# Where a softmax is divided: on TensorE and VectorE after the weighing, or on GpSimd before the transposes

## The reference

```
x  = x + attention(layernorm(x) -> q, k, v; mask 1) @ w_ao + b_ao
x  = x + attention(layernorm(x) -> q; context -> k, v; mask 2) @ w_co + b_co
x  = x + gelu(layernorm(x) @ w1 + b1) @ w2 + b2
attention: scores = q k^T / sqrt(32);  scores = scores * mask - 10000 * (1 - mask)
           probs = softmax(scores);  out = probs @ v        (16 heads of 32 channels)
```

## Time and profile before

| | us |
|---|---|
| median of three runs | 1862.97 |
| span of the profiled execution | 1856.0 |
| PE busy (share of the span) | 1736.2 (94%) |
| DVE busy | 1216.0 (66%) |
| ACT busy | 1071.9 (58%) |
| POOL busy | 99.5 (5%) |

### The profile page before, as it was taken

The page is one execution under the profiler, slowest core; times in us unless marked ns, Lnnn a source line. Parts: engine busy times, 40 slices in busy tenths (PEclk is TensorE's granted clock), DMA queues, the critical chain, the costliest instruction groups (busy, mean ns, idle before and its releaser), DMA issues.

```text
span 1856.0 us, 34276 instructions
## 1 busy us (share of the span) xinstructions
PE 1736.2 (94%) x12832; PEld 1244.6 (67%) x12832; DVE 1216.0 (66%) x2792; ACT 1071.9 (58%) x2333; POOL 99.5 (5%) x79
## 2 busy tenths in 40 slices
PE   4879999999999988999999989999999889999999
PEld 2324343444434333788888878888888779999998
DVE  5666776767776552488887887888887753333332
ACT  2346666756666574587778777777777731111111
POOL 1110101101000000000000000000000000000000
PEclk7779999999999898999999999999999999999999
DMA  6322223222222222566656766666665340000000
GB/s 160 120 82 61 91 85 97 69 92 89 81 70 66 80 61 85 140 160 167 173 149 177 196 170 189 175 174 174 172 166 154 114 144 23 23 24 23 26 28 16
DMA packets 168334, 201.73 MB, mean 109 GB/s; under 512 B 25573, under 2 KB 115813, under 8 KB 168169
## 3 DMA queue, kind: packets, MB, share of 16 engines
q1 hardware_dynamic: 167880, 199.14, 38.2%
q10 hardware_dynamic: 288, 0.39, 0.1%
HBM read 131.84 MB, written 67.63 MB: 107 GB/s over the span
## 4 chain that ended last, share of the span: by engine, by line
PE 81%; DVE 9%; ACT 5%; issue 2%; DMA 1%; DVEq 1%; ACTq 0%; SPq 0%; POOL 0%
PE c_d L2099 10%; PE c_sums L2114 9%; PE b_d L1361 9%; PE b_d L1373 9%; PE a_d L501 6%; PE b_d L1440 5%; PE a_escore L472 5%; PE a_d L579 3%; PE a_d L571 3%; PE a_mscore L484 3%; PE b_score L1428 3%; PE a_d L555 3%; PE b_d L1457 3%; DVE a_mx L804 2%; PE a_d L563 2%
## 5 line engine op out<-in xcount | busy, mean ns | idle before, releaser
L804 DVE TENSOR_REDUCE a_mx<-a_mscore 128x2 f32<-128x1024 f32 x247 | 301.9, 1222 | 170.6 <-PE a_mscore L484 169.2
L641 ACT ACTIVATE a_pt<-a_escore 128x1024 f32<-128x1024 f32 x256 | 262.5, 1025 | 164.2 <-PE a_escore L472 163.7
L1590 ACT ACTIVATE b_pr<-b_t,b_nmax 128x256 f32<-128x256 f32 x512 | 254.4, 501 | 124.7 <-DVE b_nmax L1766 124.7
L1762 DVE TENSOR_TENSOR b_t<-b_score,b_mask 128x1024 f32<-128x1024 f32 x128 | 155.1, 1212 | 85.6 <-PE b_score L1428 85.2
L2198 ACT ACTIVATE c_gT<-c_d,c_b 128x256 f32<-128x256 f32 x128 | 53.7, 472 | 267.4 <-PE c_d L2099 267.4
L1766 DVE CUSTOM_DVE_ANT_0 b_t<-b_t,b_minus 128x256 f32<-128x256 f32 x512 | 187.5, 422 | 16.8
L472 PEld LDWEIGHTS a_escore<-a_qst,a_kst 50*128 50x128 f32 x512 | 49.9, 191 | 180.7 <-ACT a_pt L641 106.1
L472 PE MATMUL a_escore<-a_qst,a_kst 50*128 50x512 f32 x512 | 133.2, 516 | 24.9 <-ACT a_pt L641 23.9
L2243 DVE CAST c_g_high<-c_gT 128x512 fp32r<-128x512 f32 x64 | 40.2, 629 | 172.0 <-ACT c_gT L2198 172.0
L2099 PE MATMUL c_d<-c_ln_high,c_w_high 128*128 128x256 f32 x512 | 144.7, 283 | 2.3 <-DVE c_ln_low L2245 2.3
L2099 PE MATMUL c_d<-c_ln_high,c_w_low 128*128 128x256 f32 x512 | 144.9, 283 | 0.0
(11 more groups left out here) (165 smaller groups left out, 3271.3 us busy)
## 6 DMA issues: line engine op xcount, KB each, us to landing
b_qst<-b_q SPq DMA_DIRECT2D x96, 256.0 KB, 4.8
b_kst<-b_k SPq DMA_DIRECT2D x96, 256.0 KB, 6.4
b_q<-b_qparts SPq DMA_DIRECT2D x64, 256.0 KB, 4.5
b_k<-b_kparts SPq DMA_DIRECT2D x64, 256.0 KB, 3.4
a_qst<-a_q_parts SPq DMA_DIRECT2D x192, 64.0 KB, 2.2
a_kst<-a_k_parts SPq DMA_DIRECT2D x186, 64.0 KB, 2.2
a_k_parts<-a_kparts SPq DMA_DIRECT2D x32, 256.0 KB, 2.3
a_q_parts<-a_qparts SPq DMA_DIRECT2D x32, 256.0 KB, 2.3
```

Of the source, the lines that this page charges most:

```text
L641: nc.scalar.activation(pt[:, at % RING, :, :], escore[:], ACT.Exp, scale=SCALE).then_inc(exp_done.sem, 1)
L804: nc.vector.tensor_reduce(mx[:, q, 2 * pair:2 * pair + 2], maxima_bank(b, n)[:], AX_X, ALU.max).then_inc(max_done.sem, 1)
L1590: last = nc.scalar.activation(pr[:, u % 2, j, :], t[:, u % 2, j, :], ACT.Exp, scale=-1.0, bias=nmax[:, u, j:j + 1], accum_out=esum[:, u, j ...
```

## The change

`divide` no longer divides, and `weigh` no longer spreads the reciprocals. Instead POOL multiplies the exponentials of each unit by the reciprocal of their row's sum, in place in `pr`, before PE transposes them. PE's transposes now wait for this (`weights_done`) and not for the exponentials. `invert` moves from the end of a DVE position to its start: invert(p+1) now stands ahead of soften(p+2). A placeholder keeps the SBUF layout as it was.

```diff
@@ gpsimd
-            for v in range(LAST + 1):
-                rsqrt(v + 2)
+            def weights(v, u):
+                if not there(v):
+                    return
+                pool.wait_ge(inverse_done.sem, inverse_done.at(v, u + 1))
+                nc.gpsimd.tensor_tensor(pr[:, u % 2], pr[:, u % 2], inverse[:, u, :].unsqueeze(2).broadcast_to([P, G, S]),
+                                        ALU.mult).then_inc(weights_done.sem, 1)
+
+            def position(v, p):
+                if p == 1:
+                    rsqrt(v + 2)
+                weights(*unit_at(v, p + 1))
...
@@ tensor, turn_probs
-                pe.wait_ge(exp_done.sem, exp_done.at(v, u + 1))
+                pe.wait_ge(weights_done.sem, weights_done.at(v, u + 1))
@@ tensor, weigh
-                for x in range(2):
-                    u = 2 * pair + x
-                    pe.wait_ge(inverse_done.sem, inverse_done.at(v, u + 1))
-                    for j in range(G):
-                        mm = nc.tensor.matmul(at[j * DH:(j + 1) * DH, (2 + x) * P:(3 + x) * P],
-                                              inverse[:, u, j:j + 1].broadcast_to([P, DH]), ident[:],
-                                              start=True, stop=True, tile_position=(0, j * DH))
@@ vector, divide
-                nc.vector.tensor_copy(spread[:], at[:, 2:4, :])
-                nc.vector.drain()
-                nc.vector.tensor_tensor(cx[:, 2 * h:2 * h + 2, q * P:(q + 1) * P], at[:, 0:2, :], spread[:],
-                                        ALU.mult).then_inc(cx_done.sem, 1)
+                nc.vector.tensor_copy(cx[:, 2 * h:2 * h + 2, q * P:(q + 1) * P], at[:, 0:2, :]).then_inc(cx_done.sem, 1)
@@ vector, position
             def position(v, p):
+                invert(*unit_at(v, p + 1))
                 soften(*unit_at(v, p + 2))
...
-                invert(*unit_at(v, p + 1))
```

More of the change, by code:

```diff
@@ L1004, in attention_layer @@
         cxp = sb("cxp", [P, 2, KT, S], F32R)
-        spread = sb("spread", [P, 2, P])
+        sb("over_ident", [P, 2 * P])
         masks_ = [[sb(n + "1", [P, TT, S])] for n in ("mask", "minus")]
@@ L1076, in attention_layer @@
         inverse_done = sig("inverse_done", NU)
+        weights_done = sig("weights_done", NU)
         cx_done = sig("cx_done", NU // 2)
@@ L1339, in _ @@
             nc.gpsimd.memset(ones[:].bitcast(F32), 1.0).then_inc(bias_set.sem, 1)
-            for v in range(LAST + 1):
-                rsqrt(v + 2)
+            def weights(v, u):
[8 more added lines that the diff above has]
+                weights(*unit_at(v, p + 1))
+            weights(0, 0)
+            for v in range(END):
+                for p in range(NU):
+                    position(v, p)
+            second["gpsimd"] = position
         @block.tensor
@@ L1456, in weigh @@
                             head = (h * HH + four * G + j) * DH
-                            nc.tensor.matmul(at[j * DH:(j + 1) * DH, x * P:(x + 1) * P], val[v % 2][:, k, head:head + DH],
-                                             pt[:, slot(v, u), k, j * P:(j + 1) * P],
-                                             start=(k == 0), stop=(k == TT - 1), tile_position=(0, j * DH))
-                for x in range(2):
-                    u = 2 * pair + x
-                    pe.wait_ge(inverse_done.sem, inverse_done.at(v, u + 1))
-                    for j in range(G):
-                        mm = nc.tensor.matmul(at[j * DH:(j + 1) * DH, (2 + x) * P:(3 + x) * P],
-                                              inverse[:, u, j:j + 1].broadcast_to([P, DH]), ident[:],
-                                              start=True, stop=True, tile_position=(0, j * DH))
+                            mm = nc.tensor.matmul(at[j * DH:(j + 1) * DH, x * P:(x + 1) * P], val[v % 2][:, k, head:head + DH],
+                                                  pt[:, slot(v, u), k, j * P:(j + 1) * P],
+                                                  start=(k == 0), stop=(k == TT - 1), tile_position=(0, j * DH))
                 mm.then_inc(pv_done.sem, 1)
@@ L2056, in _ @@
         def _(pool):
+            ahead = second["gpsimd"]
+            for p in range(4):
+                ahead(END, p)
             pool.wait_ge(consts_in.sem, 16 * 5)
@@ L2059, in _ @@
             nc.gpsimd.drain()
+            ahead(END, 4)
             def steps(b, first=False):
@@ L2064, in steps @@
                 nc.gpsimd.tensor_tensor(rstd[:], vare[:], half[:].broadcast_to([P, TT]), ALU.pow).then_inc(rstd_done.sem, 1)
+                if first:
+                    for p in range(5, POSITIONS):
+                        ahead(END, p)
                 pool.wait_ge(xn_done.sem, xn_done.at(b, 1))
```

## The result

The changed kernel takes **1985.62 us** (median of 4 runs, 1984.55 to 1986.25) against 1863.7 for the kernel before on the same chip (4 runs, 1859.38 to 1864.87): a ratio of 1.0661, 95% interval 1.0644 to 1.0677, so 122 us slower. 2013 was forecast, range 1955 to 2075.

A forecast was written before the change was run, and what follows sets the result against it. PE bounds the kernel before; afterwards a DVE-ACT loop does: 127 x 6.14 = 780, plus 35 and 19, makes 834 against 683.6, +150. Span 1856.0 becomes 2006, plus 7 gives 2013 us, range 1955 to 2075.

The forecast's parts named there:

- The loop: Part b: early reciprocal makes DVE's masking and reductions and ACT's exponentials work in turn, 5.04 us a unit without contention.
- The block: DVE's reductions, reading two SBUF inputs, are held until POOL's multiplication ends; the loop becomes 6.14 us a unit.
- E + 2.70: End of POOL's multiplication, counted from E, the end of a unit's exponentials: 0.30 us to its start plus 2.40.
- 6.14: Microseconds a unit takes in the DVE-ACT loop with reductions held by POOL; counted 127 times, 780 us.
- worse: takes longer: Rival, chance 0.15: POOL's in-place multiplication takes longer than 2.40 us; at 3.40, 2140 us in total.
- not near 2.4 us: Sign of being wrong: POOL's multiplication, priced at 2.40 us, has another duration.
- Late unit 2: POOL multiplies unit 2 only after `rsqrt`, which waits for DVE's variance: 2.5 us a round, 14 rounds, 35 us.
- the contested place: DVE's reductions for unit 4 meet POOL's ready product of unit 3; POOL going first costs 2.5 us a round, otherwise 0.9.
- PE's clock and late scores: After idling for unit 2, PE runs at its lower clock and scores come late: 0 to 1.8 us a round, taken as 0.
- Rounds of the same length: Sign in the profile after: self and cross rounds both about 51 us, since PE no longer sets their length.
- Weight splits: In five places `invert` stands behind the splitting, which joins the loop: 3.8 us each, 19 us.
- The spreading matmuls' 28 us: PE drops 64 pairs x 0.44 = 28 us of spreading matmuls, worth nothing because PE then waits.

The follow-up runs named there:

- x_loop: Kernel before, with only `invert` moved from the end of a DVE position to its start, no product on POOL: 1880.68 us, ratio 1.0096.
- x_half: Changed kernel, with POOL multiplying only 2 of the 4 heads of a unit, the others left undivided: 1943.8 us, ratio 1.0434.
- x_three: Changed kernel, with POOL multiplying 3 of the 4 heads of a unit, one left undivided: 1956.3 us, ratio 1.0500.
- x_rsqrt: Changed kernel, with POOL at position 1 multiplying unit 2 ahead of `rsqrt` and not behind it: 1947.77 us, ratio 1.0458.
- x_last: Changed kernel, with `invert` back at the end of the DVE position, POOL still dividing: 2035.53 us, ratio 1.0924.
- x_last_look: x_last run once more with nothing changed, for a trace at PE's usual clock: 2036.08 us.

## Why the prediction was right, and where its terms were off

- **The loop** (5.04 us unblocked): right. x_loop's steps are 5.03 to 5.07 where nothing else is in the way, and in the changed kernel, where the scores and so the masking come late and POOL is through before the reductions, the next step is 5.07 in most rounds.
- **The block**: right in kind, shown by x_half and x_three. **Its size was off**: I took 2.40 us from an addition whose two inputs both advance along the row and read it as good "also with a broadcast input"; but there a row of 512 values is used twice, while here one value stands for 256, and the product takes 1.90. That makes E + 2.20 in place of E + 2.70, and the step came out at 5.62 in place of 6.14, and 127 x 0.52 = 66 us less than forecast. No rival had a price below 2.40 ("worse: takes longer"), and the 0.3 us of error that I allowed for the 6.14 is less than these 0.52. An operation "not near 2.4 us" was one of my signs of being wrong, and it came.
- **Late unit 2**: the order at the contested place is right (POOL first). I forecast 2.5 us a round over regular steps, but self rounds are 48.4 to 49.8 against 8 x 5.62 = 45.0, so 3.4 to 4.8 us. The missing part is **PE's clock and late scores**, which I named, priced at 0 to 1.8 us and then set to 0. Of the 2.96 us that the masking at 1056.33 waits, the slower matmuls make 2.7, and 1.5 us in the round with the step of 9.06. x_rsqrt takes the whole place away and gains 38 us.
- **Rounds of the same length**: wrong. The five cross rounds from the second on take 265.7 us, so 53.1 each, 8.2 over regular steps. PE still sets their first step, by its wait for `b_encp` ahead of the q projection (2.87 us at 1288.88) and by what the projection then takes. That step was 7.80 us before, longer than 6.14 even then, which the average of 5.4 us a position hid; the lower clock and the held reduction bring it to 9.83.
- **Weight splits**, 3.8 us each: too high. The steps with a split are 11.11, 10.12, 8.84, 8.29 and 8.81 us. Two of them are 3.2 and 2.7 over a regular one, the first and the last lie in steps that are long without a split, and 10.12 is 4.0 over the 6.15 of that place, but the late unit 2 of the same round then costs next to nothing (5.95 in place of 9 to 10.5). In this one, at 1095.58, the splitting itself (two SBUF inputs) meets unit 2's product and takes 4.05 us in place of 2.36. It holds POOL up too, which takes 2.75:

```profile
1095.58 4.05 DVE L1695 TENSOR_TENSOR b_wq<-b_stage,b_wq 128x1024 fp32r<-128x1024 f32 x2
```

- **Sum.** 127 x 5.62 = 713.7, so what is not a regular step is 809.5 - 713.7 = 95.8 us, where 35 + 19 = 54 were forecast. So -66 and +42 make -24 of the 27 us between 2013 and 1985.6. The other 3 are what is left of two things: the span outside of the maskings grew by 2.5 us, and the median lies 1.2 us over the profiled span, not the 7 that I added. Two errors of opposite sign made the total look better than its terms; that much of it was luck.
- **The spreading matmuls' 28 us are worth nothing once PE waits**: borne out, though no run changes them alone. x_loop, which keeps them, and x_half, which has them not, make the same regular step (5.05 and 5.05 to 5.09). PE's busy time went up by 25 us in the changed kernel (1736.2 to 1761.7), though it has fewer matmuls to do; the rows at the lower level above are the only longer ones I found.

What stays open: that x_loop's 16 us and the rest add up is not shown: the terms share the same waits, and x_last shows that taking one away can cost more than it gives.

## What to carry to other kernels

Moving work to an idle engine cost latency twice here, in its own chain and in what it blocks. What I would try, from this one case: before doing it, add up the chain from one issue of the bounding engine to the next through the new engine (here scores to product, 4.94 us), and compare it with the *shortest* position that engine now makes (3.48), not with the mean (5.2). An engine that is busy all the time can still lose 7% by the order of its list, since others live on what it gives early. When an engine will have to stand still once a round, count what it then does at the lower clock.

## What the runs showed of the hardware that was not expected

- GpSimd's in-place multiplication with one input broadcast along the row (stride 0) takes 1.90 us for 128x1024 fp32, 1.47 for 128x768 and 1.04 for 128x512. That is about 0.18 us + 1.68 ns per value of a row, an estimate from the first and last that gives 1.47 for the second. The addition of 128x1024 with both inputs advancing along the row took 2.40; no run changes the stride alone, so that the stride makes the difference is not shown.
- Two GpSimd operations that are both ready let VectorE make one short instruction in between (3.92 us for the two, the next reduction 2.10 us in place of 0.42). Held the other way, behind a VectorE instruction with two SBUF inputs, the same product takes 2.75 to 2.92 us. The Trainium skill has this exclusion ("SBUF — State Buffer", "Who interferes with whom"); the trace agrees also for VectorE's custom reduction, 0.99 us against 0.42.
- The transposes that follow 5.61 us of idle TensorE take 1.97 us, and those after 4.08 us in x_last_look too, against 1.04: the lower level and the upper. Behind shorter idle stretches both occur. In x_rsqrt the q projection follows 3.01 us of idle time in rounds 8 to 14, and takes 3.11 us at a granted clock of 1.00 in one of them, 4.27 to 5.46 at 0.67 to 0.50 in the others; in x_loop 1.98 us are followed by 3.11 in one round and by 4.29 in another. So the idle time right before does not alone tell the level.
